# A two-layer FFN kernel: the routing list's products in three pieces among shared products, a small first load, the first silu ahead of the exponential, the first combines sooner, and the tail's products in another order

## The reference

```python
# layer 0
w, b = weights[subjects], bias[subjects]
xt = einsum('bct,bcd->bdt', x, w) + b[:, :, None]
scores = softmax(xt @ gate_w.T)
top_w, top_idx = top_k(scores, 2)
y = sum over e of dense_w[:, e] * ((silu(xt @ w1[e].T) * (xt @ w3[e].T)) @ w2[e].T)
z = silu(xt @ sw1.T) * (xt @ sw3.T) @ sw2.T
x = x + y + z
# layer 1
h = x @ W.T + scalings * ((x @ A[idx].T) @ Bm[idx].T)
x = x + q8dot(gelu(q8dot(h, w_gating[0])) * q8dot(h, w_gating[1]), w_linear)
```

## Time and profile before

| | us |
|---|---|
| three timed runs | 446.26, 447.30, 447.38 |
| median | 447.3 |
| profiled execution, its own time | 450.91 |
| its span, first to last instruction | 449.1 |
| PE busy in it | 436.1 (97%) |
| DVE, ACT, POOL busy | 310.1, 251.1, 188.7 |
| mean granted TensorE clock | 0.973 of full speed |

### The profile page before, as it was taken

How to read it: one execution, slowest core, us unless ns; L and a number is a source line. 1 busy time by engine, 2 the same in 40 slices (tenths; PEclk the granted TensorE clock), 3 DMA queues, 4 the chain that set the end, 5 groups by cost and what they waited for, 6 DMA issues and landing times.

```text
span 449.1 us, 8254 instructions
## 1 busy us (share of the span) xinstructions
PE 436.1 (97%) x2737; PEld 360.3 (80%) x2737; DVE 310.1 (69%) x736; ACT 251.1 (56%) x551; POOL 188.7 (42%) x188
## 2 busy tenths in 40 slices
PE   6999999999997999999999999999999999999996
PEld 5998888888776999999999999877657557557563
DVE  6983288899838677766666665576876867867845
ACT  3678154557612566556656554443764854855845
POOL 0001302990035444555544430572765755756120
PEclk9998589999979999999999999999999999999999
DMA  7996131000012555555555562231232422322101
GB/s 237 364 309 207 55 113 55 1 0 1 1 47 56 192 159 176 158 167 159 162 167 156 165 137 93 72 94 36 82 95 58 120 92 73 107 90 86 49 28 66
DMA packets 37399, 50.40 MB, mean 112 GB/s; under 512 B 4624, under 2 KB 30608, under 8 KB 37360
## 3 DMA queue, kind: packets, MB, share of 16 engines
q1 hardware_dynamic: 30016, 31.81, 21.6%
q0 software_dynamic: 6480, 17.70, 14.7%
q10 hardware_dynamic: 864, 0.37, 0.4%
HBM read 32.17 MB, written 17.69 MB: 111 GB/s over the span
## 4 chain that ended last, share of the span: by engine, by line
PE 90%; DVE 4%; ACT 2%; DMA 1%; POOL 1%; issue 1%; SPq 0%; DVEq 0%; ACTq 0%
PE bank L1110 18%; PE bank L1112 17%; PE bank L1111 17%; PE bank L1361 12%; PE bank L1376 5%; PE bank L1249 3%; PE bank L1144 3%; PE bank L1124 3%; PE bank L1288 2%; PE bank L1287 2%; PE bank L1269 2%; PE bank L1327 2%; PE bank L1187 2%; PE bank L1136 1%; DMA xg<-kept,perm 1%; PE bank L1270 1%
## 5 line engine op out<-in xcount | busy, mean ns | idle before, releaser
L389 POOL DMA_INDIRECT xg<-kept,perm x71 | 69.3, 976 | 95.2 <-PE bank L1249 58.6
L1361 PE MATMUL bank<-h,wg 128*128 128x512 fp8e4 x256 | 61.6, 380 | 0.2 <-ACT ff L616 0.2
L1361 PEld LDWEIGHTS bank<-h,wg 128*128 128x128 fp8e4 x256 | 22.2, 98 | 33.9 <-ACT ff L616 15.0
L1110 PE MATMUL bank<-w13h,xgl 128*128 x142 | 48.8, 344 | 0.2 <-issue 0.2
L396 POOL DMA_INDIRECT ga<-slots_out,slot x32 | 33.0, 1031 | 33.8 <-SPq L349 18.0
L941 DVE TENSOR_TENSOR hrl<-bank,hrh 128x256 fp32r<-128x256 f32 (+1 forms) x36 | 15.1, 421 | 45.5 <-ACT hrh L555 45.5
L1112 PE MATMUL bank<-w13h,xgh 128*128 x142 | 45.5, 320 | 0.0
L1111 PE MATMUL bank<-w13l,xgh 128*128 x142 | 45.5, 320 | 0.0
L614 ACT ACTIVATE gel<-bank 128x512 bf16<-128x512 f32 x64 | 40.2, 628 | 6.4 <-PE bank L1361 3.2
L1110 PE MATMUL bank<-xsh,sw13l 128*118 128x512 f32 (+1 forms) x96 | 41.4, 431 | 1.0 <-DVE xtL L699 0.7
L396 POOL DMA_INDIRECT gb<-slots_out,slot x32 | 38.1, 1191 | 9.8 <-issue 9.8
(11 more groups left out here) (190 smaller groups left out, 1210.9 us busy)
## 6 DMA issues: line engine op xcount, KB each, us to landing
slots_out<-yr SPq DMA_DIRECT2D x35, 256.0 KB, 2.1
xres<-in_x SPq DMA_DIRECT2D x7, 512.0 KB, 6.2
kept<-xtr SPq DMA_DIRECT2D x7, 512.0 KB, 3.7
out_x<-fin SPq DMA_DIRECT2D x7, 512.0 KB, 2.8
w13raw<-in_rw SPq DMA_DIRECT2D x8, 352.0 KB, 3.8
w2raw<-in_rw SPq DMA_DIRECT2D x8, 256.0 KB, 4.2
wgst<-in_wgate SPq DMA_DIRECT2D x16, 128.0 KB, 2.6
xg<-kept,perm POOLq DMA_INDIRECT x71
```

The lines of the kernel that those rows point to most:

```text
L389: pool.indirect_dma_start(out=xg[:, i % 2, j, :], out_offset=None, in_=kept, in_offset=bass.IndirectOffsetOnAxis(perm[:, 2 * i + j:2 * i + ...
L1110: pe.matmul(dst, al, bh, start=first, stop=False, skip_group_check=True)
L1361: ins = pe.matmul(bank[bk][:, :], wg8[:, kk, half, c * P:(c + 1) * P], h8[:, k, kk, :], start=(kk == 0), stop=(kk == KC - 1))
```

## The change

It has five parts.

1. **Start.** A new input `front` (44 columns: the subjects, the numbers 0 to 7, and the block shape) is the first transfer on ACT's queue; `hot` and `bd` read it and no longer the subjects' own load and the constants. The second half of group 0's tokens goes from SP's queue to ACT's. The constants come in two pieces, not three.
2. **Around the first shared products.** `shared_x_hi(0)` stands ahead of `conditioned(7)` on ACT. The first silu and the first high part stand ahead of the exponential; on DVE the first `hidden_mul` and `hidden_lo` stand ahead of the routing's work.
3. **The list** in pieces of 24, 20 and 20 products, with parts of shared products between them. On DVE, `routed_weight_lo(4)` and `(5)` each stand one place sooner. The transposes of the first gathered tiles stand sooner: step 0's ahead of the last down products' first two chunks, step 1's ahead of the third. For that, the two banks of these transposes are swapped (`bank[3 - k]`).
4. **First combines.** The order of `first_a`, `combine_b` and the last shared group's work on DVE.
5. **Tail.** In `last_down`, all products but the last chunk's of the third tile are made before the last chunk is waited for, and the last chunk's of three tiles stand together.

The diff, cut to its core:

```diff
@@ start
-            sp.dma_start(subj[:, :], subjects).then_inc(s("subj_in"), 16)
-
-            for h in range(2):
-                sp.dma_start(xres[:, 2 * h:2 * h + 2, :], x_t[0][:, 2 * h:2 * h + 2, :]).then_inc(x_first[h], 16)
+
+            sp.dma_start(xres[:, 0:2, :], x_t[0][:, 0:2, :]).then_inc(x_first[0], 16)
...
-            act.dma_start(cst[:, C_BLK:C_PACK], consts[:, C_BLK:C_PACK]).then_inc(s("const_in"), 16)
+            act.dma_start(front[:, :], front_in).then_inc(s("front_in"), 16)
+            act.dma_start(xres[:, 2:GT, :], x_t[0][:, 2:GT, :]).then_inc(x_first[1], 16)
             act.dma_start(cst[:, 0:C_BLK], consts[:, 0:C_BLK]).then_inc(s("shapes_in"), 16)
             act.dma_start(gatew[:, :, :], gate).then_inc(s("gate_in"), 16)
-            act.dma_start(cst[:, C_PACK:C_COLS], consts[:, C_PACK:C_COLS]).then_inc(s("shapes_in"), 16)
+            act.dma_start(cst[:, C_BLK:C_COLS], consts[:, C_BLK:C_COLS]).then_inc(s("const_in"), 16)
...
+            shared_x_hi(0)
             conditioned(7)
             keep_xT(6)
-            shared_x_hi(0)
...
             routed_weight_hi(0)
+            act.wait_ge(kept_early, 16 * (GROUPS - 2))
+            shared_silu(0, 0)
             routed_weight_hi(1)
+            shared_h_hi(0, 0, first=True)
             act.wait_ge(s("m_sub"), 1)
             act.activation(r2[:, :, :], r1[:, :, :], ACT.Exp).then_inc(s("m_exp"), 1)
-            act.wait_ge(kept_early, 16 * (GROUPS - 2))
-            shared_act(0, first=True)
+            shared_act(0, chunks=(1, 2))
...
+            hidden_mul(0, 0)
             dve.wait_ge(s("logit_psum"), GROUPS)
...
+            hidden_lo(0, 0)
...
             dve.tensor_scalar(perm[:, :], ...
+            routed_weight_lo(4)
             hidden_mul(5, 1)
-            routed_weight_lo(4)
+            routed_weight_lo(5)
             hidden_lo(5, 1)
-            routed_weight_lo(5)
...
@@ PE, the list
-            for i in range(1, EARLY - 1):
+            for i in range(1, EARLY - 2):
...
+            shared_up(EARLY - 2, parts=range(2, 6))
+            shared_down(EARLY - 2, chunks=range(2))
+            shared_up(EARLY - 1, parts=[0])
             pe.wait_ge(s("m_sub"), 1)
-            listed()
+            listed(0, 24)
+            shared_up(EARLY - 1, parts=[1])
+            listed(24, 44)
+            shared_down(EARLY - 2, chunks=[2])
+            listed(44, ENTRIES)
             shared_up(EARLY - 1, parts=range(2, 6))
-            shared_down(EARLY - 1, chunks=range(2))
...
+            pe.wait_ge(s("h_ready"), EARLY * 3 - 1)
+            routed_T(0, 0, True)
+            shared_down(EARLY - 1, chunks=range(2))
             pe.wait_ge(s("h_ready"), EARLY * 3)
-            routed_T(0, 0, True)
+            routed_T(1, 1, True)
             shared_down(EARLY - 1, chunks=[2])
-            routed_T(1, 1, True)
...
@@ PE, last_down
+                for c in range(HC - 1):
+                    pe.wait_ge(s("act8_ready"), g * HC + c + 1)
+                    product(c, 0, 6, 0)
+                    product(c, 1, 6, 1)
+                for c in range(HC - 1):
+                    product(c, 2, 7, 0)
+                pe.wait_ge(s("act8_ready"), g * HC + HC)
+                product(HC - 1, 0, 6, 0)
+                product(HC - 1, 1, 6, 1).then_inc(s("down_done"), 1)
+                product(HC - 1, 2, 7, 0).then_inc(s("down_done"), 1)
                 for c in range(HC):
...
+                    ins = product(c, 3, 5, 0)
```

More of the change, by code:

```diff
@@ L65, in tiles_of, with adaln_ffn @@
     return min(2, USED_TILES - 2 * i)
-def adaln_ffn(nc, subjects, adapters, consts, table, x, gate, sw13, sw2, rw13, rw2, l1w, scal, wgate, wlin, out, kept, slots_out):
+def adaln_ffn(nc, front_in, adapters, consts, table, x, gate, sw13, sw2, rw13, rw2, l1w, scal, wgate, wlin, out, kept, slots_out):
     x_t = x.rearrange("(g j p) f -> g p j f", j=GT, p=P)
@@ L479, in _, with shared_silu, shared_h_hi, shared_act @@
             act.activation(sw2h[:, :, :].rearrange("p a b -> p (a b)"), sw2st[0:SC, :], ACT.Copy).then_inc(s("sw_hi"), 1)
+            shared_x_hi(0)
             conditioned(7)
             keep_xT(6)
-            shared_x_hi(0)
             keep_xT(7)
             shared_x_hi(1)
-            def shared_act(i, buffers=hidden_s, first=False, between=()):
-                sil, hsf, hsh, _ = buffers
-                for c, (_, rows) in enumerate(SCH):
-                    b = c % 2
-                    act.wait_ge(s("g_done"), i * 3 + c + 1)
-                    if c >= 2:
-                        act.wait_ge(s("h_ready"), i * 3 + c - 1)
-                    act.activation(sil[0:rows, b, :], bank[b][0:rows, :], ACT.Silu).then_inc(s("sil_ready"), 1)
-                    act.wait_ge(s("h_ready"), i * 3 + c + 1)
-                    if c == 0 and not first:
-                        act.wait_ge(s("z_done"), i * 2)
-                    act.activation(hsh[0:rows, c, :], hsf[0:rows, b, :], ACT.Copy).then_inc(s("hh_ready"), 1)
+            def shared_silu(i, c, buffers=hidden_s):
+                sil, b, rows = buffers[0], c % 2, SCH[c][1]
+                act.wait_ge(s("g_done"), i * 3 + c + 1)
+                if c >= 2:
+                    act.wait_ge(s("h_ready"), i * 3 + c - 1)
+                act.activation(sil[0:rows, b, :], bank[b][0:rows, :], ACT.Silu).then_inc(s("sil_ready"), 1)
+            def shared_h_hi(i, c, buffers=hidden_s, first=False):
+                _, hsf, hsh, _ = buffers
+                b, rows = c % 2, SCH[c][1]
+                act.wait_ge(s("h_ready"), i * 3 + c + 1)
+                if c == 0 and not first:
+                    act.wait_ge(s("z_done"), i * 2)
+                act.activation(hsh[0:rows, c, :], hsf[0:rows, b, :], ACT.Copy).then_inc(s("hh_ready"), 1)
+            def shared_act(i, buffers=hidden_s, chunks=range(3), between=()):
+                for c in chunks:
+                    shared_silu(i, c, buffers)
+                    shared_h_hi(i, c, buffers)
                     if between:
@@ L544, in routed_x_hi @@
                 n = tiles_of(i) * KC * P
-                act.activation(xgh[:, k, 0:n], bank[2 + k][:, 0:n], ACT.Copy).then_inc(s("xr_hi"), 1)
+                act.activation(xgh[:, k, 0:n], bank[3 - k][:, 0:n], ACT.Copy).then_inc(s("xr_hi"), 1)
             def routed_silu(i):
@@ L1175, in ranks, with listed @@
                           start=False, stop=True, skip_group_check=True).then_inc(s("r_rank"), 1)
-            def listed():
-                for c in range(ENTRIES):
+            def listed(c0, c1):
+                for c in range(c0, c1):
                     pe.wait_ge(s("r_lanes"), c + 1)
```

59 lines of the change are left out of this document (27 added, 32 removed).

## The result

The changed kernel takes 441.33 us (median of 5, 440.23 to 442.52), the kernel before 447.38 in the same comparison (446.26 to 448.17). The ratio is 0.9877, with a 95% interval from 0.9844 to 0.9911: by the ratio 5.5 us sooner, between 4.0 and 7.0. The forecast was 436.5 with a range from 432.0 to 443.5. The profiled execution took 442.12 us with a span of 440.3, against 450.91 and 449.1.

A forecast was written before the change was run, and what follows sets the result against it. PE, busy for 436.1 of 449.1 us, was taken to bound the kernel. The terms summed to 14.6 us, taking the profiled 450.9 to 436.3; weighed with the timed median, the forecast was 436.5 us, range 432 to 443.5.

The forecast's parts named there:

- the first fall stays: Rival: the low clock from 41.5 to 58.5 us remains, 7.0 us leaves the sum, about 441 us; chance 0.19.
- Both stated signs of being wrong: Clock at 0.50 anywhere behind 41 us, or step 0's gather holding PE for more than 1 us.
- The first fall of the clock: Group 0's shared products, 41.5 to 58.5 us: the clock stays full, worth 7.7 us, net 7.0, bounds 0 and 7.7.
- What is late next: Group 0: two more table loads on ACT delay the second silu; the second down chunk waits 0.7 us.
- The list: The 64 list products, in three pieces, end at 124.4 us instead of 125.8: gain 1.4 us.
- The second fall gone: Low clock from 123.4 to 130.2 us, during the list, disappears: gain 2.0 us, bounds 0 and 2.0.
- the list's gain is eaten: Rival: PE stands at step 0's transposes, or the clock falls in the pieces; stage gives 2 for 5.5, 440 us; chance 0.10.
- slower: Rival: step 0's gather wait passes 2 us and the clock falls at 130 us, some 8 us, 449 us total; chance 0.03.
- The gather of step 2: PE's 2.02 us wait goes because step 0's transposes stand 24 down products further ahead: gain 1.3 us.
- The combines: First combines: the fourth `combine_b` ends before PE's transposes, removing the `xm` wait: gain 0.8 us, bounds 0.3 and 0.9.
- The tail: Last down products: 11 instead of 20 follow the last chunk's wait: gain 0.3 us, bounds 0 and 0.8.
- The start and the first shared products: Sooner `hot` gains 0.3 us; `shared_x_hi(0)` ahead of `conditioned(7)` removes PE's wait for `xtL`, gaining 0.7 us.

The follow-up runs named there:

- experiment 1: The kernel before, run and profiled again with no edit: 444.77 us.
- experiment 8: The changed kernel with the list in one row again, its waits standing once ahead of the 64 products: 439.14 us, ratio 0.9866 to the kernel before.
- experiment 9: The kernel before with one edit, the list's waits standing once ahead of its 64 products: 436.51 us, ratio 0.9807.
- second pair: Traces of the kernel before and the changed kernel, each profiled again without edit: 444.77 us and 439.82 us by the timed medians.
- Experiment 5: The changed kernel with the gathered tokens' transposes behind the down products, as in the kernel before: 437.22 us, ratio 0.9836.
- experiment 12: The kernel before with the list in three pieces alone, each product with its own waits: 439.36 us, ratio 0.9869.
- experiment 6: The changed kernel with VectorE's order around the first four combines as before: 441.07 us, ratio 0.9894.
- experiment 3: The changed kernel with the router's exponential ahead of the first silu again, ScalarE and VectorE in their old order there: 437.38 us, ratio 0.9846.
- experiment 7: The changed kernel with the last down products in the order of the kernel before: 439.57 us.
- experiment 2: The changed kernel, run and profiled again with no edit: 439.82 us, ratio 0.9861 to the kernel before.

## Why the prediction was right and where it failed

The direction was right for the reason given in the middle of the kernel: the list's products were held up by their waits, and weaving them in brought the list forward and took the clock fall out of it. The number lies in the range by the range's width. It stands beside the 441 of the rival "the first fall stays", and that is luck: no fall stayed, there was mostly none to lose. Both stated signs of being wrong came true at the gather of step 0.

- *The first fall of the clock, 7.0 us net.* This is the step that failed. Its mechanism was argued from one execution. In the profiled pair the term is 6.00, near the forecast; but a further trace of the same kernel has no such fall, and of 60 other executions one has a mean clock as low (experiment 1). In the usual execution the early silu is worth -0.2 to -0.3. I had put down the second reading (439.7 if the timed runs lacked the fall) and then forecast between the two. That reading was right, and a profile 3.5 us above the slowest of the times shown was evidence enough to weigh it first. (24 by 0.20 is 4.8 and not 4.7; nothing hangs on it.)
- *What is late next: 0.7 us for the second down chunk.* It was 1.46. The second silu came sooner than I had it (49.63, not 51.4), but `hsl` took 1.21 us and the next routing step 1.51, where 0.69 and 0.42 are usual, both while GpSimd was making weight splits. Exp first has two waits there, 0.49 and 0.46, so the net loss is small.
- *The list, 1.4 us.* The reason was right (experiments 8 and 9), and 1.4 was too little: 2.67 in the trace. The list ends 8.45 us behind group 5's up products, sooner even than the 8.6 that I had as the best case.
- *The second fall gone, 2.0 us.* It went from the list, and another came 9 us later, 3 us long, behind the wait of 2.19. That is the rival "the list's gain is eaten", with PE standing at the transposes and 24 down products behind them; it was underweighted at 0.10, and it ate 2.6 us of a gain that was larger than forecast (6.57 us are left in the second pair of traces, 3.91 in the first). It is also how the rival "slower" was to begin, a wait of more than 2 us and a fall behind it; the fall lasted 3 us, not the 17 of its price. My sum had the gather landing even with PE's need, 15.3 us behind the start of group 5's up products. PE was there at 14.25, since the list ended 1.3 sooner than forecast, and the tiles at 16.4: `perm` was in time (10.65 us behind that start, 10.9 forecast), but I had counted 4.4 us from there to the landing, and it took 5.8. The issues of step 0's two gathers took 1.54 and 1.48 us, where they took 1.16 and 0.94 before; why is not shown. Experiment 5 gives the price, 2.6 us.
- *The gather of step 2, 1.3 us.* The outcome is as forecast: no wait for it, and 0.41 for step 0's hidden rows (0.7 expected). The reason given, that its transposes stand 24 down products further ahead, was not needed: the wait is gone in experiments 9 and 12 as well, where they stand as before.
- *The combines, 0.8.* 1.03 by experiment 6 and the second pair; the first profile had a hold-up of 2 us there that stays unexplained.
- *The tail, 0.3.* Wrong in sign in the traces (0.5 to 1.5 us later than in the kernel before, of which 0.44 up to the last store's issue is the order's), and nothing in the medians. The step that failed is the one from the last product to the last store: I had counted the copy's 0.2 to 0.5 as won, while the first copy moved back by 0.66, and the copies, sums and stores that follow it stand in one row.
- *The start and the first shared products, 1.0.* 1.37, and 1.31 in the second pair.

The terms as the second pair of traces has them (1.3 - 0.3 + 6.6 + 1.0 - 1.4) give 7.3 us. The medians differ by 6.1 and 4.8 us; the trace of before in that pair is of an execution 2.5 us above its median, with a longer fall behind 116 us.

The Trainium skill (TensorE: Matmul & The Clock Gate, Part 4: PE-mode transpose) spoke for the first fall to stay. The changed kernel's clock is 1.00 there in both its traces, but so is that of the kernel before in experiment 1, with its longer stretch of transposes, so the runs here can't show the rule at work. The three table loads took 1.28 us each in the changed kernel, at 42.98, 46.61 and 48.34, with the next function at once behind; the 2.66 us of the Trainium skill (ScalarE: Activation LUTs, What ACT_TABLE_LOAD costs) did not show.

## What to carry to other kernels

Before a stall or a low clock in one profiled execution is given a price, it is to be set beside the timed runs: where the profile is slower than all of them, the term may be in none of them. A row of small products behind a wait each runs at the pace of the waits; one wait for all of them, where the data are there anyway, was worth more here than weaving the row into other work. And what comes sooner must be followed to the next engine: with the transposes ahead of the down products, a sooner list ended in a wait for the gather (2.2 us in the changed kernel, 3.07 in experiment 8); with the transposes behind, it ended at VectorE's row of weight splits.

## What the runs showed of the hardware

- Two satisfied waits ahead of a matrix product of 128x72 cost more than the product: 64 take 2.25 us with waits once and 7 us with a pair ahead of each. Of the 7 us, the first 20 products, which were queued, take 1; the other 44 take 0.13 us each, at 2.4 and at 1.2 GHz alike as far as the rows tell, against 0.035 with waits once. What a single wait costs was not tried. The product's own time in the rows, some 0.2 us, says nothing of that pace.
- Whether the clock falls is not the same from one execution to the next. PE stood 2.2 us for the gather and the clock then fell to 1.2 GHz in both traces of the changed kernel and in those of experiments 3, 6 and 7; in experiment 8 PE stood 3.07 us at the same place and the clock stayed at 2.4 GHz in the profiled execution. The mean clock of the changed kernel's six runs in experiment 2 goes from 0.996 to 1.000, their spans from 438.4 to 436.4 us.
- The third of three stores on SP's queue took 0.86 to 0.93 us to issue in five traces with the new tail and about 0.45 in four, where the kernel before had 0.34. In three of those four the end comes 0.8 us sooner as well. With the old tail in the changed kernel (experiment 7) it took 0.34 us again, and the end still came 0.8 us later than in the kernel before. What decides wasn't tried.
